# Last stage of an attention and FFN kernel: tokens of a chunk taken in stride four

## The reference

```
x = x + attn(layernorm(x))
x = x + ffn_fp8(layernorm(x))

attn:  q, k, v = x @ Wqkv + b                        per head
       y_softmax = causal softmax attention(q, k, v)
       state_t = retention * state_(t-1) + Gamma * (v_t k_t^T);  y_stp = (W_static + state_t) q_t
       alpha = sigmoid(gelu(x @ gate_w1 + b1) @ gate_w2 + b2)      per token and head
       y = alpha * y_softmax + (1 - alpha) * y_stp
       return y @ out_w + out_b
ffn:   x and w are quantised to fp8 with one scale over the whole tensor, multiplied, scaled back
```

## Time and profile before

| | us |
|---|---|
| median of 3 runs | 2045.02 |
| lowest and highest run | 2041.37, 2049.36 |
| span of the profiled execution | 2045.7 |
| prologue | to 185.7 |
| attention and recurrence | to about 1879 |
| last stage, first pass | about 1879 to 1971 |
| last stage, second pass | about 1971 to 2045.7 |

### The profile page before, as it was taken

The page is one execution under the profiler, slowest core; times in us unless marked ns, Lnnn a source line. Parts: engine busy times, 40 slices in busy tenths (PEclk is TensorE's granted clock), DMA queues, the critical chain, the costliest instruction groups (busy, mean ns, idle before and its releaser), DMA issues. The chain is left out here.

```text
span 2045.7 us, 43648 instructions
## 1 busy us (share of the span) xinstructions
PE 1737.9 (85%) x12880; PEld 609.5 (30%) x12880; DVE 1670.2 (82%) x1904; ACT 1435.6 (70%) x3028; POOL 1282.9 (63%) x1864
## 2 busy tenths in 40 slices
PE   5994588999998999999989999999999998886733
PEld 3441122222333222223332222233322222222622
DVE  4334999999898899998979999989898999531877
ACT  2541068889886879888868898888788888773221
POOL 2002058778784778788828887878266669990536
PEclk9996589999999899999989999999999999977865
DMA  4888132222121422311313223122321112102702
GB/s 129 196 200 187 21 80 65 70 65 86 50 71 52 94 59 69 93 60 54 88 39 90 61 71 91 59 70 74 56 65 58 51 32 77 60 26 71 189 10 73
DMA packets 142269, 159.18 MB, mean 78 GB/s; under 512 B 63184, under 2 KB 90832, under 8 KB 142032
## 3 DMA queue, kind: packets, MB, share of 16 engines
q1 hardware_dynamic: 139648, 154.55, 28.9%
q10 hardware_dynamic: 2384, 1.77, 0.3%
HBM read 117.80 MB, written 38.01 MB: 76 GB/s over the span
## 5 line engine op out<-in xcount | busy, mean ns | idle before, releaser
L1139 ACT ACTIVATE probs<-PS 128x512 f32<-128x512 f32 (+3 forms) x2304 | 1151.0, 565 | 258.3 <-PE PS L1042 189.5
L1186 DVE TENSOR_REDUCE pmax<-PS 128x2 f32<-128x1024 f32 (+3 forms) x1152 | 1232.8, 1123 | 100.2 <-PE PS L1011 83.2
L1042 PE MATMUL PS<-Q_st,K_st 50*128 50x512 f16 (+3 forms) x1408 | 436.4, 371 | 35.0 <-ACT probs L1139 11.3
L950 POOL TENSOR_TENSOR pairs<-pairs,v_exp 128x256 f32<-128x256 f32 x256 | 195.3, 763 | 324.1 <-ACT pairs L1146 322.9
L1011 PE MATMUL PS<-K_st,Q_st 48*128 48x512 f16 (+3 forms) x1408 | 338.6, 365 | 44.6 <-DVE pmax L1186 41.0
L1063 PE MATMUL PS<-probs,V_g 128*17 128x512 f32 (+3 forms) x2816 | 356.2, 580 | 0.0
L942 POOL TENSOR_TENSOR v_exp<-v_exp,k_rows 128x512 f32<-128x512 f32 x256 | 324.4, 1267 | 2.9 <-issue 2.9
L1042 PE MATMUL PS<-Q_st,K_first 50*128 50x512 f16 (+3 forms) x896 | 285.5, 384 | 23.0 <-DVE shift L1201 7.5
L1011 PE MATMUL PS<-K_first,Q_st 48*128 48x512 f16 (+2 forms) x896 | 234.7, 418 | 69.5 <-DVE pmax L1186 49.5
L1223 DVE TENSOR_TENSOR_SCAN two_steps<-retention_sq,pairs 128x257 f32<-128x257 f32 x256 | 241.3, 943 | 51.2 <-POOL pairs L954 51.2
L1042 PEld LDWEIGHTS PS<-Q_st,K_st 50*128 50x128 f16 x1408 | 119.3, 94 | 405.8 <-ACT probs L1139 332.2
(11 more groups left out here) (147 smaller groups left out, 1322.8 us busy)
## 6 DMA issues: line engine op xcount, KB each, us to landing
v_exp<-qkv_t SPq DMA_DIRECT2D x256, 256.0 KB
qkv_t<-proj SPq DMA_DIRECT2D x24, 512.0 KB, 3.7
qk_parts<-parts SPq DMA_DIRECT2D x16, 512.0 KB, 5.4
Q_st<-qk_parts SPq DMA_DIRECT2D x192, 32.0 KB, 3.2
v_rows<-vaug SPq DMA_DIRECT2D x32, 136.0 KB, 6.6
xin<-x SPq DMA_DIRECT2D x8, 512.0 KB, 6.7
k_rows<-qkv_t SPq DMA_DIRECT2D x16, 256.0 KB, 3.9
q_rows<-qkv_t SPq DMA_DIRECT2D x16, 256.0 KB, 4.5
```

The source lines that it names most:

```text
L950: pool.tensor_tensor(pairs[:, n % 2, 1:], pairs[:, n % 2, 1:], v_exp[:, n % RING, 1:CH:2], ALU.add)\
L1042: mm = pe.matmul(PS[:, bank, 0:CH - r * P], keys[rows, pair, kt * P:(kt + 1) * P], Q_st[rows, c, pair, r * P:CH], start=True, stop=(kt < T ...
L1139: act.activation(probs[:, tile % P_SLOTS, h, 0:CH - r * P], PS[:, step[5], 0:CH - r * P], ACT.Exp, scale=SCORE_SCALE).then_inc(exp_done, 1)
L1186: dve.tensor_reduce(pmax[:, s % 2, pair * TPC + j:GH * TPC:PAIRS * TPC, blk], PS[:, bank:bank + SIDES, 0:width], AX.X, ALU.max).then_inc(m ...
```

## The change

In the last stage the tokens of a chunk are laid out otherwise: partition p holds tokens 4p to 4p + 3 of the chunk instead of tokens p, 128 + p, 256 + p and 384 + p. For `xres` and `out` a partition's four rows are then one run of 4 KB in DRAM instead of four runs of 1 KB. For `soft` they are one run of 1 KB in DRAM instead of four of 256 B, while in SBUF each of the four head groups still lands as four pieces of 256 B, because the groups stand side by side in a token's row. The `stp` load is as before, and its transposes read every fourth column; so does the gate's matmul in the prologue. Two semaphore increments on SP's own queue are added.

```diff
-                            mm = pe.matmul(PS[:, 6, j * H:(j + 1) * H], gate_t[:, par, j * P:(j + 1) * P],
+                            mm = pe.matmul(PS[:, 6, j * H:(j + 1) * H], gate_t[:, par, j:CH:TPC],
                                            w2_sb[:, :], start=True, stop=True)
...
-            x_tiles = x.rearrange("(t p) n -> p t n", p=P)
-            soft_tiles = y_soft.rearrange("g (t p) v -> g p t v", p=P)
-            out_tiles = out.rearrange("(t p) n -> p t n", p=P)
+            x_rows = x.rearrange("(n p j) d -> p n (j d)", p=P, j=TPC)
+            soft_rows = y_soft.rearrange("g (n p j) v -> g p n (j v)", p=P, j=TPC)
+            out_rows = out.rearrange("(n p j) d -> p n (j d)", p=P, j=TPC)
...
+            def chunk(it, par):
+                return bass.ds(it * 2 + par, 1)
...
                             sp.wait_ge(diff_made, it * 2 + par + 1)
                             sp.wait_ge(stp_turned, it * 2 + par + 1)
+                            sp.sem_inc(beats, 1)
                             for g in range(NG):
-                                sp.dma_start(soft[:, par, :, g * GH * HD:(g + 1) * GH * HD], soft_tiles[g, :, tiles(it, par), :])\
+                                sp.dma_start(soft[:, par, :, g * GH * HD:(g + 1) * GH * HD], soft_rows[g, :, chunk(it, par), :])\
...
-                            sp.dma_start(xres[:, par], x_tiles[:, tiles(it, par), :]).then_inc(x_again[par], 16)
+                            sp.dma_start(xres[:, par], x_rows[:, chunk(it, par), :]).then_inc(x_again[par], 16)
...
                             sp.wait_ge(out_made, it * 2 + par + 3)
-                            sp.dma_start(out_tiles[:, tiles(it, par), :], o_f[:, par]).then_inc(out_stored[par], 16)
+                            sp.sem_inc(beats, 1)
+                            sp.dma_start(out_rows[:, chunk(it, par), :], o_f[:, par]).then_inc(out_stored[par], 16)
...
-                                                  stp[:, par, half, j * P:(j + 1) * P], ident[:, :])
+                                                  stp[:, par, half, j:CH:TPC], ident[:, :])
```

## The result

The changed kernel takes 2054.56 us (median of 6 runs, 2049.05 to 2055.49), the kernel before on the same chip 2045.32 us (6 runs, 2041.37 to 2049.36). The ratio is 1.0041, with a 95% interval of 1.0029 to 1.0053: slower by 0.41%, inside the 0.5% that I had set as the bound, and 0.6 us above the predicted range, which ended at 2054 us.

A forecast was written before the change was run, and what follows sets the result against it. Bounds: TensorE and DMA in the prologue; DMA, then VectorE, then VectorE and GpSimd in the last stage; attention unchanged. Terms -0.4 - 0.2 + 0.1 + 0.3 + 0.2 = 0.0 us, median 2045.0 us, range 2038 to 2054.

The forecast's parts named there:

- rival 1: Gate and transposes: strided weight load at half pace, 0.22 us instead of 0.11; about +4 us, 2049 us; chance 0.23.
- I take 5 ns, the only measured price of a stride: Strided weight loads, gate and transposes: 5 ns more per load of 128 columns, from a moving operand with step two.
- 64 x 5 ns = +0.3 us: Prologue, gate's matmul: 64 strided weight loads at 5 ns each add 0.3 us, if none hides under the DMA.
- The transposes' +0.1 us: Last stage: 16 strided loads exposed in the first and third chunks' transposes add 0.1 us; the others have room.
- rival 2: Mainly the gate: a strided column costs what four do; later chunks lose about 0.5 us each; +18, 2063 us; chance 0.06.
- `soft`, no saving: Last stage, `soft` loads: SBUF's 256 B pieces still set the packet, 2144 small packets a chunk again; saving 0.
- rival 3: Last stage loads: `soft` goes in packets of 1 KB; -3.5 us, 2041.5 us; chance 0.08.
- a load whose two sides have different runs: Sign of being wrong: such a load moves more slowly than one whose sides agree, so the `stp` waits grow.
- term of -0.4 us for `xres`: Last stage: 4 KB packets for `xres` of two chunks, ahead of the third `stp` load, save 0.4 us.
- The last store: End of the kernel: the last `out` store in 4 KB packets, estimated 170 ns each, lands 0.2 us sooner.
- SP's increments, +0.2: SP's queue: a few instructions of about 0.05 us, ahead of waiting loads and the last store, add 0.2 us.

The follow-up runs named there:

- experiment 3: Kernel before with a chunk's four gate matmuls reading at steps of 1, 2, 3 and 4 columns, and bf16 `r_t` at step four; no total time given.
- last stage alone: Changed kernel with the gate's matmul put back to contiguous columns; 2046.18 us, ratio 0.9999 to the kernel before; repeat 2043.79 us.
- `soft` alone: Kernel before with only the `soft` loads changed to runs of 1 KB of DRAM; 2045.43 us.
- gate alone: Kernel before with only the gate's matmul reading every fourth column; 2055.3 us, ratio 1.0036; repeats 2055.97 and 2058.68 us.
- experiment 5: Repeats for more traces: changed 2056.17 us, before 2045.02, before with only the gate strided 2055.97 and 2058.68, changed with the gate put back 2043.79.
- experiment 6: Kernel before with the gate's four contiguous matmuls of a chunk issued twice, no stride; 2051.56 us, ratio 1.0031; further traces 2054.06 and 2052.70 us.
- experiment 4: Kernel before with one last-stage part changed: `soft` loads 2045.43 us, `xres` and `out` 2046.48, `stp` transposes at step four 2043.80.
- experiment 1: Change split in two: kernel before with only the gate's matmul strided, ratio 1.0036; changed kernel with that matmul put back, 0.9999.

## Why the prediction was wrong

That the time would change by less than 0.5% held, with 0.41%, but not for the reasons given: the sum said 0.0 us, and the medians say +9.2 (the ratio +8.4). The range failed too: 2054.56 us lies above its end of 2054, which stood for rival 1 with nothing hidden.

**The weight load's price failed.** The step is "I take 5 ns, the only measured price of a stride" and the term made with it, "64 x 5 ns = +0.3 us". The price came from a moving operand with a step of 8 bytes. For that step it was right, for the stationary operand as well: 198 ns beside 192. It was carried over to a step of 16 bytes, and there a load costs 0.12 us more. The two medians that I had said would show it, 220 ns at the transposes and 329 at the gate, are both beyond the 10 ns allowed there. This is the mechanism of rival 1, with 0.24 us a load at the gate where it said 0.22; I had given it a chance of 0.23. By the rule of the Trainium skill on the page SBUF — State Buffer, section on the DMA port swizzle, two hits on a 16-byte line suffice: steps of 4 and 8 bytes should be equal and 16 bytes slow, and the trace agrees (192, 198, 330 ns). The step of 12 bytes, 261 ns, lies between, where a line holds 1.33 columns in the mean; that the lines are the cause is not shown, as said at experiment 3.

**Rival 1's sum was too small.** It held half of 8.8 us to be hidden, +4. The gate's part is 8 chunks by 0.97 us, 7.8 us. What came through can be read where the clock agrees: in the traces with 0.96 between 42 and 165 us the prologue ends at 182.6, 180.9 and 181.3 us with contiguous loads (before, last stage alone, `soft` alone) and at 185.7 and 186.9 with strided ones (gate alone, changed), +4.7 us, 60% of 7.8. The DMA queue, which was to hide half, has a share of 0.88 in that stretch before and of 0.83 and 0.77 with strided loads (experiment 5): it is less full when the prologue is longer. Over all traces it is more (the kernel of experiment 3, with loads of four kinds, is left out):

| loads of the gate | traces | prologue ends, us | mean | granted clock, 42 to 165 us |
|---|---|---|---|---|
| contiguous, 8 a chunk | 8 | 180.9 to 185.7 | 183.0 | 0.93 to 0.96 |
| strided, 8 a chunk | 5 | 185.7 to 193.8 | 189.8 | 0.89 to 0.96 |
| contiguous, 16 a chunk | 3 | 189.3 to 193.5 | 191.6 | 0.89 to 0.93 |

+6.8 us in the mean, since in the late prologues TensorE runs at half the clock for longer. That was in no term. Experiment 6 shows that more time on TensorE is enough for both parts: at an equal clock of 0.93 the prologue ends at 189.3 us with 16 contiguous loads and at 185.7 and 184.5 with eight, +4.2 us, and the rest comes at 0.89 and 0.90. The 1 to 2 us between these 6.8 and the timed loss of the gate alone (0.36% is 7.4 us, the medians differ by 8.5) are not placed: attention, with unchanged code, took 1695.2 us in the mean of the five strided traces and 1692.9 in the eight others, but 1693.1 in the three with 16 loads.

**The transposes' +0.1 us: right in size.** The load does cost more there, 220 ns for 163, but of that 0.05 us is exposed for eight pairs. What rival 2 had for the later chunks didn't come, the period is 9.24 us.

**`soft`, no saving: right on the packets, wrong on the path.** As many packets are under 512 B as before (63184 in the whole page), so rival 3 falls. But the claim that the change of DRAM's side costs nothing fails: the issue on SP takes 0.17 us more. It is the warning of the last part of the prediction, "a load whose two sides have different runs": the transfer isn't slower (issue to landing 2.8 us in the median, 3.3 before), but the issue is. In all six traces with the new `soft` load `x1` of the first chunk starts 24.3 to 25.6 us after the addition, behind a projection that runs in part at half the clock; in the eleven with the old one eight times at 21.8 to 22.8 and three times, again behind such a projection, at 24.4 to 25.4. Means of 24.9 and 23.0: some 1.9 us, and 94.1 against 92.0 us for the whole first pass. The means of the whole pass hold the two slow last projections of experiment 4 as well, one on each side. The issue accounts for 0.7 us of the 1.9: by so much later the third `stp` is issued in every trace with the new load, counted from the chunk's first `soft` issue (experiment 4), and the third transposes start at 18.5 us in the mean instead of 17.9. The rest goes with the clock, which in these six traces is still at half during part of the projection; that the later issue is the cause of this is argued, not tested apart. The term of -0.4 us for `xres` ahead of the third `stp` is buried under that; in the one trace that has it alone, `x1` starts at 21.8 us, earlier than in any other. The timed comparison of the last stage alone, 0.9999 with ±3 us, neither confirms nor excludes the 1.9.

**The last store: right.** 3.0 to 3.1 us from issue to the end instead of 3.4, -0.3 us for the forecast -0.2; a 4 KB packet takes at most 165 ns for the estimated 170.

**SP's increments, +0.2, and the second pass:** the second pass takes 71.1 to 71.5 us in all traces. Nothing is seen of them.

## What to carry to other kernels

Here a stationary operand of 128 fp32 columns read with a step of 12 or 16 bytes took 0.07 and 0.14 us longer to load, one with a step of 8 bytes 6 ns. Where 128 columns were moved behind each load, nearly all of it was hidden; where 16 were, each load held TensorE up by 0.12 us, and more than half of that reached the end of the prologue. So put the columns in order in the write before it, which cost ScalarE nothing here. Don't take a strided price from another step: the nearest row was no bound. And a transfer is more than its packets: when the two sides are cut differently, look at the time of its issue. A single trace per kernel would have misled here, as experiment 1 shows: the prologue of one program ended at 185.7 us in one trace and at 193.8 in another.

## What the runs showed of the hardware

- One program has traces whose clock falls in different places. The prologue of the kernel before had a granted clock of 0.93 and 0.96 and ended at 185.7 and 182.6 us. The ten timed runs of the gate alone stand in two groups, three at 2043.7 to 2048.3 us and seven from 2053.9 on. Why the clock stays at half for longer when TensorE is later in each chunk is open: the rows say only at which level it was in a stretch.
- A single fall can cost 2 to 3 us where VectorE waits for TensorE: before `x1` of the first chunk (24.6 against 22.4 us with the same code) and in the last projection (6.49 against 3.72 us, the wait behind it 4.14 against 1.37).
- ScalarE reads PSUM in steps of four elements in 687 ns, the time for neighbours.
